# A gated cross-attention and mixture block on one core: three hand-placed steps moved in the programs of ScalarE, GpSimd, VectorE and TensorE

## What is computed

```python
def xattn(query, key_in, value, group_prob, mask, ...):
    logits = einsum('bhqd,bhkd->bhqk', q, k) / sqrt(dh) + (1 - mask) * -1e9
    attn = softmax(logits) * group_prob
    return merge_heads(attn @ v) @ wo + wo_b
def ffn(h):
    normed = h * rsqrt(mean(h * h) + 1e-8) * norm_weight
    shared = relu(normed @ sw1 + sb1) @ sw2 + sb2
    scores, idx = top_k(sigmoid(normed @ router_w.T), 2)
    w = scores / (sum(scores) + 1e-6)
    routed = sum over the two experts e of w_e * (relu(normed @ ew1[e] + eb1[e]) @ ew2[e] + eb2[e])
    return shared + routed
x = x + tanh(g_xattn) * xattn(layernorm(x), ctx, ctx, fside, mask, ...)
x = x + tanh(g_ffn) * ffn(layernorm(x))
```

## Time and profile before

| | |
|---|---|
| median of three executions | 659.84 us |
| their spread | 658.57 to 664.95 us |
| the profiled execution | 662.9 us |
| its span, first to last instruction | 661.1 us, 1.8 us of the time lying around it |
| mean granted PE clock | 0.944 of 2.4 GHz |
| PE busy, PEld busy | 583.0 us (88%), 490.9 us (74%) |
| DVE, ACT, POOL busy | 435.1, 429.8, 311.7 us |
| DMA | 84.29 MB, 127 GB/s mean |

### The profile page before, as it was taken

The page is one execution under the profiler, slowest core; times in us unless marked ns, Lnnn a source line. Parts: engine busy times, 40 slices in busy tenths (PEclk is TensorE's granted clock), DMA queues, the critical chain, the costliest instruction groups (busy, mean ns, idle before and its releaser), DMA issues.

```text
span 661.1 us, 18993 instructions
## 1 busy us (share of the span) xinstructions
PE 583.0 (88%) x6006; PEld 490.9 (74%) x6006; DVE 435.1 (66%) x1182; ACT 429.8 (65%) x1071; POOL 311.7 (47%) x357
## 2 busy tenths in 40 slices
PE   2679999999999999999958894799999999999950
PEld 2347888888888888888747781588888888888840
DVE  5957888888888888888985651245555536536327
ACT  4367888888888888888847531347565656656330
POOL 8303655544444447763360177143476555558120
PEclk9898999999999999999986896799999999999995
DMA  8724657776565566734110042021544643552228
GB/s 230 177 72 104 171 138 192 207 201 151 144 150 150 149 151 154 166 93 138 63 64 2 12 149 104 24 79 38 155 151 120 193 119 104 129 159 56 57 71 311
DMA packets 106777, 84.29 MB, mean 127 GB/s; under 512 B 42915, under 2 KB 100517, under 8 KB 106606
## 3 DMA queue, kind: packets, MB, share of 16 engines
q1 hardware_dynamic: 103694, 75.59, 43.5%
q0 software_dynamic: 3040, 8.16, 3.4%
HBM read 50.45 MB, written 28.30 MB: 119 GB/s over the span
## 4 chain that ended last, share of the span: by engine, by line
PE 61%; issue 8%; ACT 6%; DVE 6%; POOL 5%; DMA 4%; SPq 1%; POOLq 0%; ACTq 0%; DVEq 0%
PE ps L1204 15%; PE ps L1177 14%; PE ps L1028 10%; PE ps L1046 5%; PE ps L945 5%; PE ps L1015 5%; PE ps L976 4%; ACT probs L804 3%; POOL w L661 2%; ACT ctxT L728 2%; DMA probs<-x_sent 2%; POOL w L659 2%; DVE probs L1351 1%; DVE x_sb L1588 1%; PE ps L1170 1%
## 5 line engine op out<-in xcount | busy, mean ns | idle before, releaser
L1028 PE MATMUL ps<-ident,probs 112*125 112x112 f32 x768 | 193.1, 277 | 1.1 <-ACT arena L795 0.5
L804 ACT ACTIVATE probs<-probs,negmax 112x375 f32<-112x375 f32 x256 | 154.4, 606 | 12.6 <-DVE negmax L1351 12.1
L863 ACT ACTIVATE arena<-ps,b 128x256 f32<-128x256 f32 x192 | 79.5, 464 | 123.2 <-PE ps L1177 108.9
L1028 PEld LDWEIGHTS ps<-ident,probs 112*125 112x125 f32 x768 | 139.5, 188 | 22.4 <-issue 9.2
L1204 PE MATMUL ps<-w,arena 128*128 128x256 f16 x1152 | 136.6, 278 | 12.1 <-issue 10.7
L1351 DVE CUSTOM_DVE_ANT_0 probs<-ps,neg 112x375 f32<-112x375 f32 x256 | 136.8, 540 | 5.0 <-issue 1.3
L1520 DVE TENSOR_TENSOR arena<-arena 128x512 f16<-128x512 f32 x96 | 74.6, 785 | 96.1 <-ACT arena L868 86.8
L1204 PEld LDWEIGHTS ps<-w,arena 128*128 128x128 f16 x1152 | 113.7, 99 | 31.5 <-issue 16.2
L1363 DVE TENSOR_TENSOR arena<-ps,gpT 125x336 f32<-125x336 f32 x192 | 97.1, 506 | 39.8 <-PE ps L1028 35.9
L561 POOL TENSOR_TENSOR probs<-probs,gp_in 112x375 f32<-112x375 f32 x64 | 58.7, 917 | 133.2 <-ACT probs L804 132.6
L1177 PE MATMUL ps<-probs,w 128*128 x816 | 92.1, 273 | 1.0 <-issue 0.4
(11 more groups left out here) (176 smaller groups left out, 800.8 us busy)
## 6 DMA issues: line engine op xcount, KB each, us to landing
kst<-k_scratch SPq DMA_DIRECT2D x64, 140.6 KB, 3.7
w1s<-in_L_ffn_ew_dram SPq DMA_DIRECT2D x8, 1024.0 KB
w2s<-in_L_ffn_ew_dram SPq DMA_DIRECT2D x8, 1024.0 KB, 5.7
x_sent<-y_sb SPq DMA_DIRECT2D x12, 516.0 KB, 6.0
ctx_in<-in_ctx_dram SPq DMA_DIRECT2D x16, 375.0 KB
k_scratch<-kT SPq DMA_DIRECT2D x32, 187.5 KB, 2.5
arena<-y_back SPq DMA_DIRECT2D x7, 512.0 KB, 6.9
k_scratch<-kT SPq DMA_DIRECT2D x32, 93.8 KB, 2.0
```

What stands on the lines that cost most here:

```text
L804: act.activation(probs[:, n % PROBS], probs[:, n % PROBS], ACT.Exp, bias=negmax[:, p, n:n + 1], scale=-1.0, accum_out=rowsum[:, p, ORDER[n ...
L863: act.activation(hid32[:, f], ps[:, f // 2 % 4, f % 2 * TILE:(f % 2 + 1) * TILE], ACT.Relu, bias=b1[:, f, e:e + 1]).then_inc(h_relu, 1)
L1028: mm = pe.transpose(ps[0:KP, PT[n % 2], c * S:(c + 1) * S], probs[:, n % PROBS, c * KP:(c + 1) * KP], ident[0:S, 0:S])
```

## The change

There are three moves; no instruction that computes is added or removed.

- ACT evicts CTX1 after the first exponential of a step instead of after the second (n == 0, was n == 1), in 14 steps.
- POOL runs `spread_inverse(15)` after three weightings instead of ahead of all.
- DVE chooses the experts after it has split tile 0's hidden values, not ahead of it, and makes the slots after it has split tile 1's. PE runs tile 0's `results`, then tile 1's `hidden`, then the ranks, then tile 1's `results`. The loop on PE covers tiles 2 to 5.

```diff
@@ gpsimd @@
             step(B - 1, 1, B // 2, None, more=False, last=True)
-            spread_inverse(B - 1)
...
             for i in range(NT):
+                if i == 3:
+                    spread_inverse(B - 1)
                 if i == 2 * (H - PJ_FROM) - 2:
                     split_out(B - 1)
@@ scalar @@
-                    if t_next and not first and n == LEAD - 3:
+                    if t_next and not first and n == LEAD - 4:
                         prep_piece(t + 1, CTX1, 1 - p)
@@ tensor @@
-            rank_pairs()
             pe.wait_ge(w2_lo, 1)
             results(0, 0)
-            with pe.Fori(1, ST - 1) as i:
+            hidden(0, shared_rows(1))
+            rank_pairs()
+            results(1, 0)
+            with pe.Fori(2, ST - 1) as i:
                 shared_tile(i)
@@ vector @@
-            dve.wait_ge(rl_mm, NT)
-            dve.wait_ge(sum_zero, E + 3)
...
-            choose(logit, 0)
...
+            def choose_experts():
+
+                dve.wait_ge(rl_mm, NT)
+                dve.wait_ge(sum_zero, E + 3)
+                choose(logit, 0)
...
             then(dve.tensor_scalar(sb2_bc[:, :], sb2_bc[:, :], gates[:, 1:2], None, ALU.mult))
-            shared_tile(0)
+            split_hidden(0)
+            choose_experts()
+            add_shared(0)
+            split_hidden(1)
             place_pairs()
-            shared_tile(1)
+            add_shared(1)
             split_up_low(1, 1)
-            shared_tile(2)
+            split_hidden(2)
+            add_shared(2)
             weigh_pairs()
             with dve.Fori(3, ST) as i:
-                shared_tile(i)
+                split_hidden(i)
+                add_shared(i)
```

More of the change, by code:

```diff
@@ L1483, in running @@
                     then(dve.tensor_tensor(to[:, pad:pad + n], src[:, pad:pad + n], src[:, pad - 2 ** k:pad - 2 ** k + n], ALU.add))
-            choose(logit, 0)
-            then(dve.scalar_tensor_tensor(rt[:, 2], rt[:, 0], -BIG, logit, ALU.mult, ALU.add))
-            choose(rt[:, 2], 1)
-            then(dve.tensor_tensor(before[:, 0, NTP:NTP + NT], rt[:, 0], rt[:, 1], ALU.add))
-            then(dve.tensor_copy(count16[:, 0], before[:, 0, NTP:NTP + NT]))
-            running(lambda k: before[:, k], NT, NTP, 4)
-            then(dve.tensor_copy(count16[:, 1], before[:, 0, NTP - 1:NTP - 1 + NT]))
-            dve.tensor_copy(count16[:, 2, 0], before[:, 0, NTP + NT - 1]).then_inc(cnt_made, 1)
-            dve.tensor_copy(xwords[:, :, 1], top[:, 2]).then_inc(word_made, 1)
+            def choose_experts():
+                dve.wait_ge(rl_mm, NT)
+                dve.wait_ge(sum_zero, E + 3)
+                choose(logit, 0)
+                then(dve.scalar_tensor_tensor(rt[:, 2], rt[:, 0], -BIG, logit, ALU.mult, ALU.add))
+                choose(rt[:, 2], 1)
+                then(dve.tensor_tensor(before[:, 0, NTP:NTP + NT], rt[:, 0], rt[:, 1], ALU.add))
+                then(dve.tensor_copy(count16[:, 0], before[:, 0, NTP:NTP + NT]))
+                running(lambda k: before[:, k], NT, NTP, 4)
+                then(dve.tensor_copy(count16[:, 1], before[:, 0, NTP - 1:NTP - 1 + NT]))
+                dve.tensor_copy(count16[:, 2, 0], before[:, 0, NTP + NT - 1]).then_inc(cnt_made, 1)
+                dve.tensor_copy(xwords[:, :, 1], top[:, 2]).then_inc(word_made, 1)
             def place_pairs():
@@ L1525, in split_up_low, with add_shared @@
                 dve.tensor_tensor(w1[:, p, LO], w1s[:, :, :], w1[:, p, HI], ALU.subtract).then_inc(w1_lo, 1)
-            def shared_tile(i):
-                split_hidden(i)
+            def add_shared(i):
                 two = bass.ds(2 * i, 2)
```

## The result

The changed kernel takes 655.98 us (median of 8 runs, 654.61 to 657.63) against 661.48 for the kernel before (658.16 to 664.95, 8 runs): 0.9924 of its time, 95% interval 0.9898 to 0.9951. That is 5.5 us faster, where the forecast had 10.2 in its sum. The profiled execution took 657.1 us with a span of 655.3, against 662.9 and 661.1.

What follows compares the result with a forecast made beforehand. PE was taken to bound an attention step, idle 0.34 of 17.57 us. Gains of 5.4 (context), 0.7 (inverse sums) and 4.1 (experts) sum to 10.2 us; 659.84 less that is 649.6, stated as 650, range 643 to 658.

Steps and rivals of the forecast that it cites:

- The context: Attention steps: evicting CTX1 sooner removes PE's wait for it, gaining 5.4 us, with 3.0 and 7.0 as ends.
- the first rival: Attention steps: PE then waits for something else, only the shared network gains; 5.8 us, 654.0 us; chance 0.2.
- The inverse sums: POOL's weightings: the output split starts 0.8 us sooner, gaining 0.7 us, with 0 and 1.2 as ends.
- The experts: Shared tile 0: results no longer wait for DVE's choosing and run at full clock; 4.1 us, ends 2.5 and 4.3.
- the clock: Tile 0's results on PE: without idle time ahead the clock stays up, 6.69 us becomes 5.24, saving 1.45 us.
- The step that failed: PE's bad stretch during the sendings, about 17 us lost: taken to move with the sendings and cost the same.
- The slack: POOL behind the 28 sendings: 16.99 us of idle time was to hide the first sending coming 3 us later.
- The slower one: PE during the sendings: the bad stretch starts with the first sending, 18 us more, 668 us; chance 0.06.
- The second: PE's shared-tile loop: bad stretch is instruction refetching, shrinks with one pass less; 633 to 645 us; chance 0.1.

Runs made afterwards that it cites:

- e4: Kernel before with the context evicted one head sooner and the inverse sums among the weightings, the experts' choosing unmoved: 636.79 us, ratio 0.9913.
- e5: Kernel before with only the context evicted one head sooner: 655.42 us, ratio 0.9901.
- q3: Kernel before with POOL's split of expert 0's second weights cut into four breaks between the sendings: 642.46 us, ratio 0.9987.
- s3: Changed kernel with POOL pausing after 14 of 28 sendings until tile 3's hidden values are split: 655.2 us in one run, before's median 662.14.
- q1: Changed kernel with two useless memsets on POOL as a break ahead of sendings 7, 13, 19 and 25: 645.99 us, ratio 0.9747.
- q2: Changed kernel with POOL's split of expert 0's second weights cut into four breaks between the sendings: 632.99 us, ratio 0.9558.
- e1: Changed kernel with PE's loop over tiles 2 to 5 written out, on a chip without the stretch: 635.36 us, ratio 0.9893.
- e2: Changed kernel with POOL's first sending held until tile 2's hidden values are split: 640.94 us in one run, before's median 641.73.
- u1: Changed kernel with PE's loop written out and SP loading expert 1's second weights behind the first two row loads: 656.0 us, ratio 0.9922.

## Why the prediction was right in its moves and wrong in its sum

**The context.** The mechanism held: the wait is gone, and no other took its place, so the first rival falls. The size was off: 5.4 forecast, (17.57 - 17.07) x 14 = 7.0 by the step of the windows, the upper end. From PE's turn of the first sequence's sums to that of the last it is 332.67 - 76.53 = 256.1 us before and 325.20 - 75.47 = 249.7 after, so 6.4 us in all, as the last two steps gain nothing; of the 7.5 us in the table the other 1.1 are there at the first sums already. I had leaned on the idle time of 0.33 us that is put down to the wait; the difference of the two starts, 0.50, was the better measure.

**The inverse sums.** 0.7 forecast; PE's wait for the split went from 2.0 to 1.1, and the gain grew from 7.5 to 8.5 us by tile 0. Of the 1.0 us in between, 0.17 only makes good what the turn of the sums now waits for the copy, so the move gave 0.8. Right.

**The experts.** 4.1 forecast, 12.5 - 8.5 = 4.0 measured, with the results at 5.40 us and the ranks without idle time, as told. In the sum 6.69, a length in PE's timeline, stood against 5.24, a length in the chain; by starts the results took 372.09 - 365.56 = 6.53 and take 5.24, so the clock gave 1.3 us and not 1.45. It doesn't give that everywhere: in e4, e5 and q3 these results take 5.40 us without move 3. That the first sending would come 3 us later against the program was right as well: 376.7 less 8.5 is 368.2, and it is at 371.3.

**The step that failed** is "If it follows the sendings, it moves with them and costs the same". It does follow them, and ends with them. But it doesn't begin with them. The earlier trace rows show PE untouched for 21.3 us, and I asked what ends the stretch and not what begins it. It begins 7.6 to 10.6 us into an unbroken row of sendings, and move 3 changed which sending stands beside DVE's 2.28 us of splitting: the seventh before, the second now. So a break that kept PE fast for eight more microseconds was thrown away, and the stretch is 7.2 us longer by the windows (27.7 against 20.5), of which tile 3 pays 6.5. These are most of what is missing: 13.6 us at tile 3 less 6.5 is 7.1. That breaks count is shown by s3, q1 and q2; that this one did is read from the timelines, as no run moves DVE's splitting alone. The last 1.1 us go in the experts' part, which takes 180.3 us from its first tile on before and 181.4 after; 1.0 of it is PE's waiting for the experts' rows, 1.2 against 0.2 us. The changed kernel's traces on chips C, D and E take 179.9 to 180.2, so I take it for scatter.

**The slack.** Also wrong was to call the later sendings free for POOL's 16.99 us of idle time. The end of the sendings is the end of the stretch, so 3 us of delay against the program lengthen it; and without a stretch the rows are late (e1: 3.8 us of waits; e2, with the sendings held: 10.6).

**The rivals.** The slower one, that the stretch begins sooner, came nearest to what happened, at a chance of 0.06: the beginning moved from 21.3 to 13.0 us behind the first sending, not to 0, and cost 6.5 us, not 18. The second, drawn from the Trainium skill, Runtime: NRT & Kernel Launch, Instruction fetch mechanics, falls by u1: with PE's loop written out, so without taken branches in these tiles, the stretch takes 29.2 us. For a kernel without the stretch the sum of 10.2 was a little low: q2 and q3 are 11.1 us apart at tile 3, with nothing from the clock in it. The same comes out of the first two traces, 13.6 less 1.1 for tile 2's wait and 1.3 for the clock is 11.2. That the ends lie 10.0 and 9.5 us apart, so near to 10.2, is in part luck, as other losses and gains meet there.

## What to carry to other kernels

When a trace has a stretch in which an engine crawls for no visible reason, find what begins it as well as what ends it, by laying several traces over each other, before assuming that it moves with something. A long row of indirect DMAs from GpSimd is better broken up with other work of that engine every six or so, on a chip that shows the stretch: here breaks of useless work took the changed kernel from 656.0 to 646.0 us (q1), and breaks of work that otherwise stood behind the sendings to 633.0 (q2). On chip B, without the stretch, such breaks gave the kernel before nothing (q3). Slack that is measured beside such a stretch is slack of the stretch, and is gone when it goes.

## What the runs showed of the hardware

**The stretch.** On four of the six chips of the experiments, and in the first comparison, PE's instructions start on ticks of 0.7 us once GpSimd has sent for 7.6 to 10.6 us without a break, and until about 3 us after it stops. PE after the change:

```profile
399.28 0.40 PE L1205 MATMUL ps<-w,arena 128*128 128x256 f16 x1 [1.03 <-issue]
400.00 0.37 PE L1205 MATMUL ps<-w,arena 128*128 128x256 f16 x1 [0.33 <-issue]
402.10 0.37 PE L1205 MATMUL ps<-w,arena 128*128 128x256 f16 x1 [1.73 <-issue]
```

The starts lie 0.72 and 2.10 us apart, one and three times 0.7. A single matmul takes 0.37 to 0.40 us here and 0.27 at the full clock earlier in the stretch; what grows is the time between them. The granted clock is no cause of it: it is still 1.00 from 384.0 to 387.8, when PE has begun to crawl, and 0.50, the 1.2 GHz level, from 387.9 to 412.0. On two chips the same sendings at the same pace do nothing to PE, and the same kernel takes 642 us in place of 661.

**What comes ahead of it.** The other engines learn late that PE is done, while PE itself still runs at full speed. PE, DVE and ACT after the change, in which L1540 adds the results of tile 2 and L864 is the first relu of tile 3:

```profile
375.43 5.40 PE L1205 MATMUL ps<-w,arena 128*128 128x256 f16 x48
380.67 3.55 PE L1178 MATMUL ps<-xnT,w 128*128 x31
```

```profile
382.37 0.48 DVE L1540 SCALAR_TENSOR_TENSOR x_sb<-ps,gates,x_sb 128x256 f32<-128x256 f32 x1 [3.69 <-PE ps L1205]
383.72 0.48 DVE L1540 SCALAR_TENSOR_TENSOR x_sb<-ps,gates,x_sb 128x256 f32<-128x256 f32 x1 [0.86 <-remote]
```

```profile
390.12 0.84 ACT L864 ACTIVATE arena<-ps,b 128x256 f32<-128x256 f32 x2 [12.76 <-PE ps L1178]
```

The results end at 375.43 + 5.40 = 380.83, and the additions start 1.5 and 2.9 us behind that; the relu starts 9.5 us behind the start of its hidden layer. The same two in e1, on a chip without the stretch, where the results end at 380.48 and the hidden layer starts at 380.32:

```profile
380.26 0.88 DVE L1539 SCALAR_TENSOR_TENSOR x_sb<-ps,gates,x_sb 128x256 f32<-128x256 f32 x2 [1.92 <-PE ps L1205]
```

```profile
381.83 0.84 ACT L864 ACTIVATE arena<-ps,b 128x256 f32<-128x256 f32 x2 [4.82 <-PE ps L1178]
```

In the kernel before, the delay comes twice: the first relu of tile 2 starts 3.9 us behind its hidden layer (386.46 against 382.57), behind the first six sendings, and beside the one that is held up the delay ends, so that no other relu of that tile waits; then that of tile 3 starts 7.2 us behind (401.40 against 394.23), and there the stretch is. So something piles up with the sendings and drains in a break. It also made the wait of 0.85 us at tile 2's results before. That PE slows when this pile is full would fit all the traces, but no run tests it.

What it is that piles up, and why two chips are free of it, stays open: the recorded instruction fetches don't show it, none lying between 379.5 and 450.4 in the changed kernel. Whether it is the time, the count or the bytes of the row that matters wasn't told apart either, since all rows had one pace and one size.

**A sending beside DVE.** It takes 2.83 or 2.18 us in place of 0.97, and ends 0.84 us (387.80 against 386.96) and 0.85 us (374.86 against 374.01) after DVE's instruction with two inputs. The Trainium skill, SBUF — State Buffer, Who interferes with whom, says that such an instruction contends with one of GpSimd that reads SBUF; the trace agrees. That such a hold-up can work as a break, and keep PE fast as it seems to have done in the kernel before, I had not expected at all.
